# Two places of VectorE's order where a fused attention kernel changes its mode

## The reference: what is computed

```
x = x + einsum('bsi,boi->bso', x, weight[adapter_ids])
q, k, v = x @ Wq.T, x @ Wk.T, x @ Wv.T              # 32, 8 and 8 heads of 128
q, k = rope(rmsnorm(q) * q_norm_w), rope(rmsnorm(k) * k_norm_w)
k_all, v_all = concat(cached[block_table], new)     # 512 + 128 keys
scores = q @ k_all.T / sqrt(128), cached keys past the length masked
x = x + (softmax(scores) @ v_all) @ Wo.T
```

## Time and profile before

| | |
|---|---|
| median of 3 runs | 1008.42 us (1005.34 to 1008.75) |
| the profiled execution's own time | 1005.44 us |
| its span | 1003.6 us |
| TensorE busy | 990.6 us (99%) |
| VectorE, ScalarE, GpSimd busy | 861.0, 808.5, 793.6 us |
| TensorE's share of the chain that ended last | 94% |
| granted TensorE clock | 1.00 |

### The profile page before, as it was taken

One profiled execution on the slowest core, in us unless ns is written; L12 is line 12 of the kernel. 1 busy time (PEld: TensorE's weight loads), 2 busy tenths in 40 slices (PEclk: granted clock), 3 DMA queues, 4 the chain that ended last, 5 costly groups with the idle time before them and its releaser, 6 DMA issues.

```text
span 1003.6 us, 19444 instructions
## 1 busy us (share of the span) xinstructions
PE 990.6 (99%) x5491; PEld 863.3 (86%) x5491; DVE 861.0 (86%) x1786; ACT 808.5 (81%) x2105; POOL 793.6 (79%) x810
## 2 busy tenths in 40 slices
PE   7999999999999999999999999999999999999998
PEld 5778888888888888888888888888888888888886
DVE  7686567689999899999998999899999989998995
ACT  4455456688889889888988898898889888988884
POOL 3886777667889779897898888898798978888672
PEclk9999999999999999999999999999999999999999
DMA  8989979889988888888978888788888888887773
GB/s 251 281 251 265 259 206 241 236 180 200 221 160 161 160 159 160 163 155 154 173 156 157 163 166 159 148 166 153 173 150 167 156 151 167 164 164 147 150 150 85
DMA packets 507436, 178.72 MB, mean 178 GB/s; under 512 B 424561, under 2 KB 489474, under 8 KB 507330
## 3 DMA queue, kind: packets, MB, share of 16 engines
q1 hardware_dynamic: 380016, 143.99, 68.7%
q10 hardware_dynamic: 126162, 31.13, 14.3%
q0 software_dynamic: 1152, 2.36, 0.9%
HBM read 104.53 MB, written 30.94 MB: 135 GB/s over the span
## 4 chain that ended last, share of the span: by engine, by line
PE 94%; SPq 2%; DVE 1%; DMA 1%; issue 1%; ACT 0%; ACTq 0%; DVEq 0%
PE S L1408 22%; PE O L1341 7%; PE O L1342 7%; PE O L1343 7%; PE Y L1341 6%; PE Y L1343 6%; PE Y L1342 6%; PE Q L1343 6%; PE Q L1342 6%; PE Q L1341 6%; PE T L1347 5%; PE KV L1342 3%; PE KV L1341 3%; PE KV L1343 3%; PE KV L1361 1%; SPq L330 1%
## 5 line engine op out<-in xcount | busy, mean ns | idle before, releaser
L1080 DVE SCALAR_TENSOR_TENSOR pr<-pr,rc,raw 128x640 f16<-128x640 f32 x216 | 252.6, 1169 | 16.4 <-ACT raw L817 16.3
L1052 DVE CUSTOM_DVE_ANT_0 pr<-S,mask,rst 128x640 f32<-128x640 f32 x256 | 225.4, 880 | 16.6 <-PE S L1408 13.5
L837 ACT ACTIVATE pr<-pr,nb 128x640 f32<-128x640 f32 x256 | 211.8, 827 | 16.6 <-DVE nb L1052 16.5
L817 ACT ACTIVATE raw<-pr,rc 128x640 f16<-128x640 f32 x216 | 172.9, 826 | 0.4 <-DVE rc L1068 0.3
L617 POOL TENSOR_TENSOR m<-m 128x512 f32<-128x512 f32 x63 | 112.0, 1778 | 72.8 <-DVE m L1119 45.1
L570 POOL TENSOR_TENSOR kl<-raw,kh 128x512 fp32r<-128x512 f32 x64 | 97.1, 1517 | 34.1 <-ACT kh L720 33.1
L1408 PE MATMUL S<-kh,qh 128*128 128x320 f32 x512 | 119.9, 315 | 3.6 <-DVE nb L1052 2.4
L591 POOL TENSOR_SCALAR ptl<-turned 128x512 fp32r<-128x512 f16 x135 | 107.7, 798 | 17.1 <-issue 5.9
L591 POOL TENSOR_SCALAR ptl<-first 128x512 fp32r<-128x512 f16 x135 | 107.9, 799 | 11.7 <-issue 0.6
L1408 PE MATMUL S<-kh,ql 128*128 128x320 f32 x512 | 116.7, 309 | 0.0
L1408 PE MATMUL S<-kl,qh 128*128 128x320 f32 x512 | 116.4, 308 | 0.0
(11 more groups left out here) (179 smaller groups left out, 2686.8 us busy)
## 6 DMA issues: line engine op xcount, KB each, us to landing
wraw<-in_wall SPq DMA_DIRECT2D x74, 256.0 KB, 4.5
cache_rows<-in_kv ACTq DMA_DIRECT2D x68, 224.0 KB, 7.3
raw<-cache_rows SPq DMA_DIRECT2D x58, 256.0 KB, 4.0
raw<-cache_rows ACTq DMA_DIRECT2D x52, 256.0 KB, 5.1
cache_rows<-in_kv SPq DMA_DIRECT2D x44, 224.0 KB, 4.0
mask<-mask_rows SPq DMA_DIRECT2D x64, 128.0 KB, 4.4
first<-in_lw SPq DMA_DIRECT2D x5, 1024.0 KB
cache_rows<-in_kv SPq DMA_DIRECT2D x16, 192.0 KB, 4.2
```

The lines of the kernel that those rows point to most:

```text
L817: e.activation(upper16[:, g, :], pr[:, slot(u, g), :], ACT.Copy, scale=rc[:, u % 2, g:g + 1]).then_inc(a_f1, 1)
L837: e.activation(pr[:, slot(u, g), :], pr[:, slot(u, g), :], ACT.Exp, bias=nb[:, u % 2, g:g + 1], scale=-1.0, accum_out=sm[:, u % 2, g:g + 1 ...
L1052: e.tensor_tensor_reduce(pr[:, slot(u, g), :].rearrange("p (a n) -> p a n", a=2), S[:, :, 0:320], mask[:, u % 2, :].rearrange("p (a n) -> ...
L1080: e.scalar_tensor_tensor(out=lower16(u, g), in0=pr[:, slot(u, g), :], scalar=rc[:, u % 2, g:g + 1], in1=upper16[:, g, :], op0=ALU.mult, op ...
```

## The change

On VectorE two pairs of neighbours change places, each once in the whole program. In period 9 `p_lo(8, 3)` and `p_lo(8, 4)` come ahead of `lower_plane(9, 0)`. In period 10 `largest(10, 1)` comes ahead of `lower_plane(9, 3)`; the last period had that order already, and the periods 11 to 62 keep the old one. No instruction is added or removed, and the other engines' orders are the same.

```diff
@@ period 9 (i == NA), first loop of the VectorE program
                 if i >= 0:
                     largest(i, 3)
-                if i == NA:
-                    lower_plane(i, 0)
                 if turn:
                     p_lo(w, 3)
                     p_lo(w, 4)
+                if i == NA:
+                    lower_plane(i, 0)
                 new_k_lo(j)
@@ period 10 (i == NA + 1), second loop
                 if nxt:
                     q_products(j)
-                if i == LAST:
+                if i in (NA + 1, LAST):
                     largest(i, 1)
                 if w < LAST:
                     lower_plane(w, 3)
-                if i < LAST:
+                if NA + 1 < i < LAST:
                     largest(i, 1)
```

## The result

The changed kernel takes 1011.65 us in the median of 20 runs (1007.40 to 1013.12), the kernel before 1008.42 in 20 (1005.27 to 1009.60). The ratio is 1.003 with a 95% interval of 1.0021 to 1.0039. It is slower by 3 us, within half a per cent, but clear of zero and above the upper end of my range, 1008.9. The forecast was a gain of 1.05 us.

What follows compares the result with a forecast made beforehand. TensorE, busy 99% of the span, was taken as the bound; gains of 0.78 and 0.27 us sum to 1.05, so the median of 1008.42 was to become 1007.4 us, range 1003.8 to 1008.9.

Steps and rivals of the forecast that it cites:

- What bounds the kernel, and where the effect lies: TensorE busy 99% of the span; only its `ptl` wait (0.51 us, period 9) and `nb` wait (0.67 us, period 10) reachable.
- Part one: Period 9, `p_lo` pair ahead of `lower_plane(9, 0)`: TensorE's `ptl` wait goes, gain 0.78 us, bounds 0.5 and 0.8.
- Its price at `kl`: The new keys' low part, behind the delayed `lower_plane(9, 0)`, holds by 0.1 us: counted 0, bound 0.2 us lost.
- VectorE's cover: VectorE's 0.99 us idle ahead of `largest(10, 0)` takes up the delay of `lower_plane(9, 1)`.
- two small ones: Two instructions in VectorE's queue between `lower_plane(9, 1)` and `add_output(7)`, listed without a size.
- Part two: Period 10, `largest(10, 1)` ahead of `lower_plane(9, 3)`: `scores(10, 2)` starts earlier, net gain 0.27 us, bounds 0 and 0.90.
- the new wait for `ol`: Period 10, in front of projection Y: TensorE waits 0.3 to 0.5 us.
- What is late next: Unit 9's lower-plane transpose lands 0.5 us later, at 219.3; GpSimd waits 0.5 us, its third `ptl` in time by 0.2.
- I count nothing, with a bound of 0.3 us: The price set for the late lower-plane transpose and GpSimd's `ptl` in period 10: nothing, at most 0.3 us.
- The rival on the slower side: Late unit 9 planes make GpSimd's `ptl` hold TensorE at period 10's end: price 0.3 to 1 us, 1009.0 us, chance 0.05.
- point of decision: Time rises only if `lower_plane(9, 3)` ends more than 1.3 us later than 215.51, after 216.8; expected at 216.0.
- Behind 232 us: TensorE stays busy throughout from 232 us on; nothing there gives the gain back or adds to it.

Runs made afterwards that it cites:

- e3: The changed kernel with ScalarE's key load of unit 12 issued earlier, between two upper planes of period 10; 1007.19 us, ratio 0.9997 to the kernel before.
- e4: The changed kernel with ScalarE's key load of unit 12 issued one instruction later in period 10; 1007.32 us, ratio 0.9997 to the kernel before.
- e9: The changed kernel with SyncE issuing nothing in period 10 behind the last lower-plane transpose until it landed; 1009.73 us, ratio 1.0039 to the kernel before.
- e1: The kernel before with only the period 9 swap, the two `p_lo` ahead of `lower_plane(9, 0)`; 1004.47 us, ratio 0.9978.

## Why the prediction was wrong

Point by point:

- **What bounds the kernel, and where the effect lies:** right. TensorE's idle time in periods 9 and 10 is all of it, and both executions need 780.0 us behind it.
- **Part one, 0.78 us:** right at its place, 0.77. The collision of `lower_plane(9, 0)` with GpSimd came with its size (1.99 us), but that it came was luck: three of seven profiles with this swap are without it. Its price at `kl` was 0.13 us, within the bound of 0.2. The clause that VectorE's cover takes the rest up failed: the scaling behind `lower_plane(9, 1)` sat 1.1 us behind GpSimd's `kl`. I had counted it among "two small ones" and asked no row what it does beside GpSimd. It cost 0.07 us at once and about half of part two.
- **Part two, 0.27 us:** the swap did start `scores(10, 2)` sooner, the new wait for `ol` came (0.26 us), the plane was second to GpSimd's sum (1.32 us) and the sum took 1.28. But with `largest(10, 1)` late its gain at the place was 0.35, and the wait took 0.52 back. Parts one and two together gave 0.40, not 1.05. In e3, without the two meetings, they gave 1.04, so the sum itself was sound up to that point.
- **"What is late next":** this is the step that failed. I took the landing of the transpose from its one row, 3.3 us, as if it belonged to the transpose, and asked only when the plane ends. The landing was 5.9, since the issue slid under a key load on another queue: the gap shrank from 2.5 to 0.46 us. "I count nothing, with a bound of 0.3 us" was 2.81 us of delay and 1.58 of slow clock. Even without the load the bound was too small: the same step lost 0.45 us in e3 and 0.52 in e4.
- **The rival on the slower side** had the right place and the right wait, at 0.05. Its point of decision was wrong for the same reason: it let the plane be 1.3 us late, and 1.1 was enough. Its price of 0.3 to 1 us left out the longer landing and the clock.
- **Behind 232 us:** no wait came, as said. That the period there has two values, 14.46 and 14.52, I had not looked for; its 3 us are the size of the step between the two groups of runs that the prediction had noticed and left unexplained.

e3 and e4 settle it from the other side: with only the key load moved, the time is back at that of the kernel before.

## What to carry to other kernels

A wait that is worth half a microsecond is not removed for nothing where a chain of planes, transfers and rounding stands behind it: follow the moved instruction to every DMA issue that it releases, and ask what other queues issue in the microseconds behind that. A landing time read from one row holds only for that row's neighbours. And when TensorE is the bound and never waits, the price of the first long wait can be the wait and then the slower clock after it: in the changed kernel's profile 1.58 us on top of 2.81, in e9's nothing.

## What the runs showed of the hardware

- A DMA transpose of two planes lands in 3.3 us when a 256 KB load from another queue is issued 2.5 us behind it, in 4.0 at 1.5 us, in 5.8 to 5.9 at 0.26 to 0.46 us, in 3.9 when it is issued 0.7 us ahead, and in 3.8 when it has already landed. In e9 nearly all of the transpose's data had moved 3.2 us after its issue; the loss lies in its last 33 packets, which ran on until the load was through, and in 1.6 us without data before the landing. Why is not shown.
- A VectorE instruction on 128 x 2 numbers can cost 1.27 us beside GpSimd. The Trainium skill (SBUF — State Buffer, "Who interferes with whom") names tensor_scalar among the operations that can take the shared port. The trace agrees: it ended 0.03 us after GpSimd's `kl`. In e3 the same instruction took 0.55 us and again ended 0.03 us after a GpSimd row.
- TensorE's clock fell to half after 2.57 us of idle time in the changed kernel's profile, and not in e9's, with a wait of the same length. In e1's profile it was 0.50 from 42 to 44 us, behind a wait of 1.23 us at 41; the kernel before, with a wait of 1.07 us there, stayed at 1.00.
- The second part of the program has two rhythms. These are TensorE's key transposes of periods 11 and 61 in e3:

```profile
234.58 0.27 PE L1527 MATMUL KV<-ident,k 128*128 128x128 f32 x1
...
960.55 0.27 PE L1527 MATMUL KV<-ident,k 128*128 128x128 f32 x1
```

  50 periods in 725.97 us, 14.52 each. In the kernel before the same two are at 235.92 and 958.95, 14.46 each, 2.94 us less in all. In both TensorE shows no wait. In the profiles of both the rhythm was kept to the end. Between neighbouring matmuls the two differ by 0.01 or 0.02 us, at some places and not at others; what sets it stays open.
